# Running counts and scores of the second pass looked up in float32 from one table

## The reference

```python
src = jnp.concatenate([_s, _d, _loop]); dst = jnp.concatenate([_d, _s, _loop])
_o = jnp.argsort(dst, stable=True); src = src[_o]; dst = dst[_o]
...
def _L1_gnn_ref(node_states, edges, kernel, kernel_attention):
    dst = edges[:, 0]                      # edges = stack([src, dst], axis=1)
    src = edges[:, 1]
    h = jnp.matmul(node_states, kernel)
    score_dst = jnp.matmul(h, a_dst); score_src = jnp.matmul(h, a_src)
    scores = jax.nn.leaky_relu(score_dst[dst] + score_src[src], negative_slope=0.2)
    scores = jnp.exp(jnp.clip(scores, -2.0, 2.0))
    scores_sum = jax.ops.segment_sum(scores, dst, num_segments=n_nodes)
    attention_norm = scores / scores_sum[dst]
    return jax.ops.segment_sum(h[src] * attention_norm[:, None], dst, num_segments=n_nodes)
```

## Time and profile before

| | |
|---|---|
| median of the runs | 12312.5 us |
| the profiled execution | 12319.95 us, its span 12318.2 us |
| stage_move in its span | about 4041 to 7355 us |
| mean granted TensorE clock | 0.804 of 2.4 GHz |
| busy in the span | PE 6923.2 us, DVE 6711.3, POOL 6398.0, ACT 1613.7 |

### The profile page before, as it was taken

One profiled execution on the slowest core, in us unless ns is written; L12 is line 12 of the kernel. 1 busy time (PEld: TensorE's weight loads), 2 busy tenths in 40 slices (PEclk: granted clock), 3 DMA queues, 4 the chain that ended last, 5 costly groups with the idle time before them and its releaser, 6 DMA issues. The chain is left out here.

```text
span 12318.2 us, 202597 instructions
## 1 busy us (share of the span) xinstructions
PE 6923.2 (56%) x43540; PEld 5743.1 (47%) x43541; DVE 6711.3 (54%) x13147; ACT 1613.7 (13%) x4982; POOL 6398.0 (52%) x7772
## 2 busy tenths in 40 slices
PE   4777777776583555555555526996467730100375
PEld 3666666665473444444444424773256630000364
DVE  5333333334677555555555525887455689600499
ACT  1000000000211322222222200111100000000011
POOL 2555555551384344444444455882166678877300
PEclk9999999999797777777777758997588865555698
DMA  3555555553373344444444459993077742344454
GB/s 98 161 159 157 161 160 159 161 159 114 106 207 92 113 129 131 129 128 132 129 130 127 139 155 179 269 268 85 28 179 192 192 123 73 92 113 108 127 168 127
DMA packets 2114487, 1742.89 MB, mean 141 GB/s; under 512 B 377268, under 2 KB 1838645, under 8 KB 2114213
## 3 DMA queue, kind: packets, MB, share of 16 engines
q1 hardware_dynamic: 1220182, 819.70, 22.8%
q10 hardware_dynamic: 708032, 472.39, 15.8%
q0 software_dynamic: 186160, 449.72, 13.0%
HBM read 1289.54 MB, written 453.29 MB: 141 GB/s over the span
## 5 line engine op out<-in xcount | busy, mean ns | idle before, releaser
L1152 POOL DMA_INDIRECT sorted<-m_rows,srci x1612 | 1574.4, 977 | 1768.6 <-ACT srci L1256 978.0
L1612 POOL DMA_INDIRECT z_xg<-table,srci x1664 | 1888.1, 1135 | 725.5 <-issue 473.3
L452 POOL DMA_INDIRECT g_xg<-table,srci x1612 | 1581.1, 981 | 1105.8 <-DVE g_es L554 628.3
L1201 PE MATMUL m_psl<-m_part,m_ohtb 128*128 128x100 bf16 x4836 | 472.1, 251 | 1175.7 <-DVE m_mul L1340 725.7
L471 PE MATMUL g_psg<-g_wg,g_eT 128*128 128x136 f32 x3224 | 1047.0, 472 | 135.3 <-issue 134.3
L1672 PE MATMUL z_ps<-z_wrow,z_oh 128*128 128x132 f32 x3712 | 575.0, 302 | 957.8 <-issue 472.2
L488 PE MATMUL g_psx<-scores,g_hot 128*128 x3608 | 840.3, 362 | 446.1 <-DVE e_score L579 267.7
L488 PEld LDWEIGHTS g_psx<-scores,g_hot 128*128 128x128 f32 x3608 | 806.5, 328 | 477.8 <-issue 476.5
L1484 PE MATMUL n_ps<-n_row,n_oh 128*128 128x257 f32 x3712 | 880.3, 389 | 192.6 <-DVE n_row L1460 170.4
L1201 PEld LDWEIGHTS m_psl<-m_part,m_ohtb 128*128 128x128 bf16 x4836 | 408.5, 123 | 1227.3 <-issue 978.0
L1672 PEld LDWEIGHTS z_ps<-z_wrow,z_oh 128*128 128x128 f32 x3712 | 488.6, 203 | 1044.3 <-issue 972.9
(11 more groups left out here) (412 smaller groups left out, 13950.8 us busy)
## 6 DMA issues: line engine op xcount, KB each, us to landing
n_row<-sorted SPq DMA_DIRECT2D x464, 520.0 KB, 4.7
z_buf<-gathered ACTq DMA_DIRECT2D x464, 256.0 KB
g_keys<-dst_row ACTq DMA_DIRECT2D x451, 256.0 KB
ag_buf<-gated SPq DMA_DIRECT2D x451, 256.0 KB, 3.2
m_keys<-dst_row ACTq DMA_DIRECT2D x451, 256.0 KB
gathered<-z_xg SPq DMA_DIRECT2D x416, 256.0 KB
gated<-g_y SPq DMA_DIRECT2D x403, 256.0 KB
g_eT<-in_attr_t SPq DMA_DIRECT2D x402, 256.0 KB
```

The lines of the kernel that those rows point to most:

```text
L452: nc.gpsimd.indirect_dma_start(out=xg[:, u, j, :], out_offset=None, in_=v.table[:, :], in_offset=bass.IndirectOffsetOnAxis(ap=v.srci[:, t: ...
L1152: nc.gpsimd.indirect_dma_start(out=v.sorted[:, :], out_offset=bass.IndirectOffsetOnAxis(ap=place[:, t:t + 1], axis=0), in_=rows[:, u, j, : ...
L1201: nc.tensor.matmul(to, ohtb[:, u, j * P:(j + 1) * P], before, start=(n == 0), stop=False)
L1612: nc.gpsimd.indirect_dma_start(out=xg[:, u, j, :], out_offset=None, in_=v.table[:, :], in_offset=bass.IndirectOffsetOnAxis(ap=v.dsti[:, t: ...
```

## The change

The three bf16 terms go. `cnt` gets a second half with the score of every node, filled once, and `lookups` multiplies a float32 copy of the transposed one-hots, `oht`, with `cnt` directly: one float32 matmul of 100 columns for a tile where there were three in bf16. `ohtb` stays for `same`. The parts `high` and `middle` go from ACT, `below_high` and `below_middle` from DVE; `turned` gets a second copy from PSUM. `lookups` now waits for `s_qm`, `s_oht`, `s_run` and `s_mul`; `counts` also waits for the second copy of the group before; `running` waits for lookups of three groups earlier.

```diff
-        cnt, mul = sb("_cnt", [P, R, G, NBX]), sb("_mul", [P, 2, G, 2, NBX])
-        part, rest = sb("_part", [P, R, 3, G, 2, NBX], BF16), sb("_rest", [P, 2, G, NBX])
+        oht = sb("_oht", [P, R, G * P])
+        cnt, mul = sb("_cnt", [P, R, G, 2, NBX]), sb("_mul", [P, 2, G, 2, NBX])
...
                     if later(g, 1):
                         pe.wait_ge(s_run, g + 1)
                         pe.wait_ge(s_ohtb, g)
+                        pe.wait_ge(s_oht, g)
...
                 def lookups(g, u, use):
                     pe.wait_ge(s_qm, g + 1)
-                    pe.wait_ge(s_ohtb, g + 1)
-                    pe.wait_ge(s_low, g + 2)
+                    pe.wait_ge(s_oht, g + 1)
+                    pe.wait_ge(s_run, g + 2)
...
-                        for n in range(3):
-                            before = part[:, u, n, j - 1, :, :] if j else part[:, (u - 1) % R, n, G - 1, :, :]
-                            nc.tensor.matmul(to, ohtb[:, u, j * P:(j + 1) * P], before, start=(n == 0), stop=False)
+                        before = cnt[:, u, j - 1, :, :] if j else cnt[:, (u - 1) % R, G - 1, :, :]
+                        nc.tensor.matmul(to, oht[:, u, j * P:(j + 1) * P], before, start=True, stop=False)
                         last = nc.tensor.matmul(to, qm[:, u, j, :], ohhi[:, u, j, :, :], start=False, stop=True)
...
                     nc.scalar.activation(ohtb[:, u, :], pst[:, :], ACT.Copy).then_inc(s_ohtb, 1)
-
-                def high(g, u, use):
...
-                    nc.scalar.activation(part[:, u, 0, :, 0, :], cnt[:, u, :, :], ACT.Copy).then_inc(s_high, 1)
+                    nc.scalar.activation(oht[:, u, :], pst[:, :], ACT.Copy).then_inc(s_oht, 1)
...
-                def middle(g, u, use):
-                    act.wait_ge(s_rest, g + 1)
-                    nc.scalar.activation(part[:, u, 1, :, 0, :], rest[:, u % 2, :, :], ACT.Copy).then_inc(s_middle, 1)
...
+                nc.vector.tensor_copy(cnt[:, :, :, 1, :].rearrange("p r t c -> p (r t) c"),
+                                      v.scores[:, None, :, 0].broadcast_to([P, R * G, NBX])).then_inc(s_fix, 1)
...
                     if later(g, R):
-                        dve.wait_ge(s_rest, g - R + 1)
+                        dve.wait_ge(s_look, g - R + 2)
                     dve.wait_ge(s_cnt, g + 1)
-                    nc.vector.tensor_tensor(cnt[:, u, :, :], tiles(psu[:, 0:G * NBX]),
-                                            cnt[:, (u - 1) % R, G - 1:G, :].broadcast_to([P, G, NBX]),
+                    nc.vector.tensor_tensor(cnt[:, u, :, 0, :], tiles(psu[:, 0:G * NBX]),
+                                            cnt[:, (u - 1) % R, G - 1:G, 0, :].broadcast_to([P, G, NBX]),
                                             ALU.add).then_inc(s_run, 1)
-
-                def below_high(g, u, use):
...
-                def below_middle(g, u, use):
...
-                pipeline(dve, GE, (hot, 3, KE), (fill, 6, KE), (below_middle, 3), (choose, 4), (onehots, 0), (running, 1),
-                         (below_high, 2), (position, 4), ring=R)
+                pipeline(dve, GE, (hot, 3, KE), (fill, 6, KE), (choose, 4), (onehots, 0), (running, 1), (position, 4), ring=R)
```

More of the change, by code:

```diff
@@ L1090, in stage_move @@
     s_oh, s_cnt, s_run, s_ohtb = (sem("r_" + n) for n in ("oh", "cnt", "run", "ohtb"))
-    s_first = sem("r_first")
-    s_high, s_rest, s_middle, s_low = (sem("r_" + n) for n in ("high", "rest", "middle", "low"))
+    s_oht = sem("r_oht")
     s_q, s_qm, s_look, s_mul, s_pos, s_place = (sem("r_" + n) for n in ("q", "qm", "look", "mul", "pos", "place"))
@@ L1195, in lookups @@
                     else:
-                        pe.wait_ge(s_fix, R + 1)
+                        pe.wait_ge(s_fix, 2)
                     for j in range(G):
                         to = psl[:, j * 2 * NBX:(j + 1) * 2 * NBX]
-                        for n in range(3):
-                            before = part[:, u, n, j - 1, :, :] if j else part[:, (u - 1) % R, n, G - 1, :, :]
-                            nc.tensor.matmul(to, ohtb[:, u, j * P:(j + 1) * P], before, start=(n == 0), stop=False)
+                        before = cnt[:, u, j - 1, :, :] if j else cnt[:, (u - 1) % R, G - 1, :, :]
+                        nc.tensor.matmul(to, oht[:, u, j * P:(j + 1) * P], before, start=True, stop=False)
                         last = nc.tensor.matmul(to, qm[:, u, j, :], ohhi[:, u, j, :, :], start=False, stop=True)
@@ L1236, in turned @@
                     nc.scalar.activation(ohtb[:, u, :], pst[:, :], ACT.Copy).then_inc(s_ohtb, 1)
-                def high(g, u, use):
-                    act.wait_ge(s_run, g + 2)
-                    if later(g, R):
-                        act.wait_ge(s_look, g - R + 2)
-                    nc.scalar.activation(part[:, u, 0, :, 0, :], cnt[:, u, :, :], ACT.Copy).then_inc(s_high, 1)
+                    nc.scalar.activation(oht[:, u, :], pst[:, :], ACT.Copy).then_inc(s_oht, 1)
                 def earlier(g, u, use):
@@ L1266, in put @@
                                          facts[:, ds(g * G, G), 1:4], ACT.Copy).then_inc(s_put, 1)
-                pipeline(act, GE, (spread, 1, KE), (turned, 2), (high, 2), (earlier, 2), (middle, 3), (index, 5), (put, 5, KE), ring=R)
+                pipeline(act, GE, (spread, 1, KE), (turned, 2), (earlier, 2), (index, 5), (put, 5, KE), ring=R)
             @block.vector
@@ L1272, in _ @@
                 nc.vector.memset(rows[:, :, :, :], 1.0).then_inc(s_set, 1)
-                nc.vector.tensor_copy(cnt[:, R - 1, G - 1, :], run[:, :]).then_inc(s_run, 1)
+                nc.vector.tensor_copy(cnt[:, R - 1, G - 1, 0, :], run[:, :]).then_inc(s_run, 1)
                 link = chain(dve, s_split)
@@ L1318, in running @@
                     if later(g, R):
-                        dve.wait_ge(s_rest, g - R + 1)
+                        dve.wait_ge(s_look, g - R + 2)
                     dve.wait_ge(s_cnt, g + 1)
-                    nc.vector.tensor_tensor(cnt[:, u, :, :], tiles(psu[:, 0:G * NBX]),
-                                            cnt[:, (u - 1) % R, G - 1:G, :].broadcast_to([P, G, NBX]),
+                    nc.vector.tensor_tensor(cnt[:, u, :, 0, :], tiles(psu[:, 0:G * NBX]),
+                                            cnt[:, (u - 1) % R, G - 1:G, 0, :].broadcast_to([P, G, NBX]),
                                             ALU.add).then_inc(s_run, 1)
-                def below_high(g, u, use):
[L1326 to L1329, removed]
-                def below_middle(g, u, use):
-                    dve.wait_ge(s_middle, g + 1)
-                    nc.vector.tensor_tensor(part[:, u, 2, :, 0, :], rest[:, u % 2, :, :], part[:, u, 1, :, 0, :],
-                                            ALU.subtract).then_inc(s_low, 1)
                 def choose(g, u, use):
```

## The result

The changed kernel takes 11918.58 us, the kernel before beside it 12309.51 us: ratio 0.9684, 95% interval 0.9671 to 0.9696, 391 us less. The forecast was 12104 with 11780 to 12330. The sign and the place were right; the gain is nearly twice the sum.

What follows compares the result with a forecast made beforehand. stage_move was taken to be bound by POOL's own time plus the stretch from PE's late signals to its next burst. Gains of 180, 15, 11 and 2.5 us (set-up) sum to 209: 12104 us, range 11780 to 12330.

Steps and rivals of the forecast that it cites:

- What bounds the kernel: In stage_move no engine is full; it pays POOL's own time plus the stretch from signal release to next burst.
- The stretch after a release: In stage_move, from PE's late signals to POOL's restart: 5.85 us, shortened by 1.45 us a release; 206 us in all.
- The hand-over as a gain by itself: DVE's choose no longer waits through L1333 for ACT's second term behind its late copy: 1.17 us a release.
- DVE's two instructions: DVE loses L1328 and L1333; L1328's 0.28 us comes off the way from choose to fill.
- The slower rival: PE's expand signal is caught behind POOL's burst, so bursts of two groups break up; 12570 us, chance 0.12.
- The count being last nearly always: At DVE's L1321 the count's signal comes last nearly always, so an earlier choose waits; 12256 us, chance 0.12.
- a sign of no gain: In stage_move: waits of DVE's L1321 for PE grown from 53.
- PE as the end of the stretch: After a release PE at 1.2 GHz ends the stretch, its longer lookups uncovered; 12310 us, chance 0.10.
- PE's price: In lookups, float32 costs 0.6 us more a step, scaled from expand by columns; covered, so nothing in the sum.
- The scatters: On POOL: with fewer two-operand DVE instructions they come back a little to 960 ns; too small to enter.
- The larger gain: Stage_move's loop leaves the burst pattern: 588 us less, 11724, or about half, 12020; chance 0.15.

Runs made afterwards that it cites:

- e1_middle_first: Kernel before with ACT's part middle moved ahead of earlier, so the second bf16 term no longer queues behind the late copy; 12129 us, ratio 0.9992.
- e3_dve_work_back: Changed kernel with two DVE subtractions of 200 columns added per step, whose results nobody reads; 12063 us, ratio 0.9937.
- r_before: Kernel before, unchanged, run for its trace on a chip without late signals; 9697 us.
- r_after: Changed kernel, unchanged, run on a chip without late signals; 9677 us, ratio 0.9972.
- e5_fill_behind: Kernel before with fill moved behind below_middle on DVE; 12156 us, ratio 1.0011.

## Why the prediction was right, point by point

*What bounds the kernel* was read rightly for that chip: bursts, late signals, and a stage that pays for POOL plus the stretch to its restart. On the fast chips there are no late signals, POOL has no wait of this kind, and the stage takes 1161 us less.

*The stretch after a release* was the mis-sized term. The sum took 1.45 us off for 124 releases and less for the rest, 206 us in all; POOL's waits for others fell by 499 us over some 205 restarts, 2.4 us each. The step that failed is that a release would find DVE at the choose, with only 1.45 us less to do. These are the stretches from the end of DVE's longest wait to POOL's restart, grouped by where DVE stood (median in us, and the number of restarts in brackets, in the steps with lookups; the 11 to 29 restarts before which DVE had no wait over 1 us are left out):

| DVE stood at | before | after | e1_middle_first | e3_dve_work_back |
|---|---|---|---|---|
| the fill | 1.6 (3) | 1.6 (116) | 1.6 (39) | 1.6 (44) |
| the counts | 3.2 (12) | 3.2 (40) | 3.8 (66) | 3.2 (109) |
| the choose | none | 4.9 (22) | 4.9 (95) | 4.7 (35) |
| the third term, L1333 | 5.4 (165) | gone | 2.4 (2) | gone |

The stretch goes with the place and is much the same in all four. For the place that the prediction assumed, the choose, it is 4.9 us where 4.4 was forecast, but that is only 22 restarts of after. In most DVE rests at the fill, with the choose and its signals behind it; a fill then follows the release at once. What the sum left out on the other side is that the release comes later after the last scatter (1.51 against 0.27 us).

That the time fell inside the range is in part luck: 11919 lies outside 12020 to 12190, to which the forecast gave 0.48, and the range reached down to it for the sake of a rival with another mechanism.

*The hand-over as a gain by itself* (1.17 of the 1.45 us) did not show on chip 7: with it gone and DVE's work left, the time is the same, and the wait stands at the next signal of PE. *DVE's two instructions* were held to be worth 0.28 us a release. Their return left a gain of 78 us, in place of what would be some 380 if 0.968 holds there; that would be 0.75 us a step for 0.72 us of busy time. That the two parts act together is what the runs suggest. Why DVE comes to rest at the fill, which of PE's signals gets out ahead of the burst, is argued and not shown.

*The slower rival* named the right event and the wrong price. PE's expand did get caught behind the burst: that is the 149 waits of the fill. But its signal was late about as often before, over 1 us in 207 of 438 records of it, after in 211 of 417; DVE had to wait at the fill for it only 13 times before, since it stood elsewhere. A step that waits had its other work done, as the text said against this rival, and the fill comes first after the release. Counted from the scatters (a stop is over 1 us of idle time), bursts of four went from 15 to 38 and bursts of eight from 158 to 145, not a quarter of them.

*The count being last nearly always* did not happen. It is the commonest place of DVE in e3_dve_work_back (129 waits at the counts, 86 at the choose, 56 at the fill). In after the waits of the counts for PE doubled from 53 to 106, which was given as a sign of no gain; the gain came all the same. *PE as the end of the stretch* did not show in the result, although PE's price was too low: tiles follow each other at 5308.81 and 5309.40, so 0.59 us at 1.2 GHz against 0.33, 1.04 us a step and not 0.6, near the upper bound. Scaling the expand row by columns was wrong: by the same rows the float32 call of 100 columns takes some 0.51 us (an estimate, 0.59 less a quarter of 0.33 for the bf16 matmul beside it), and expand with 129 columns 0.52.

*The scatters* were left out of the sum as too small, and grew by 83 us. See below.

*The larger gain* (588 us, or half) is nearer to the truth than the forecast in its size: 391 us, and half of it had been put at 12020. Its mechanism, a loop without bursts, did not come: POOL still stops some 200 times.

## What to carry to other kernels

Where several engines wait on each other in a ring, find at which instruction each of them stands when a delay ends; what counts is how much work lies between that instruction and the one that feeds the bound engine, and taking one wait away can just move the stop to the next signal. Don't take a stall that the profile puts down to "remote" for a property of the kernel until a second chip shows it: here the stage took 3314 us with it and 2153 without, and the gain was 3.2% with it and 0.25% without. Before costing work as hidden, ask by which resource it could still slow the bound engine.

## What the runs showed of the hardware

*PE's signals come late on some chips and not on others.* The trace records when a semaphore is updated, with some updates missing. In stage_move of before 787 of 1615 updates by PE came over 1 us after the end of its instruction, for "same" 179 of 394, with a median of 6.1 and at most 12.0 us, for expand at most 15.4. Of 4643 updates by ACT and DVE in the same stretch none came over 0.02 us after. In r_before and r_after all 3221 updates by PE came within 0.02 us. The windows above add that the late ones cost time in stages with POOL's indirect DMAs: in stage_move and the first stage, and not in the one behind stage_move, which has none and shows no wait for "remote". On the chips where they come, PE's own float32 instructions also come slowly at such times: in after, matmuls of L1209 begin 0.7 to 1.4 us apart.

```profile
5303.83 0.27 PE L1209 MATMUL m_psx<-held,m_hot 128*128 x1 [0.18 <-issue]
...
5305.25 0.27 PE L1209 MATMUL m_psx<-held,m_hot 128*128 x1 [1.16 <-issue]
5306.01 0.27 PE L1209 MATMUL m_psx<-held,m_hot 128*128 x1 [0.48 <-issue]
```

The ends of matmuls in the trace are modelled, so a late signal may be a late product. What delays them stays open.

*A scatter that starts early in a DVE instruction with two SBUF operands is longer.* In the release above the scatter of 1.40 us starts at 5308.47, inside L1282 (from 5308.35, 0.69 us), which reads iota and lo from SBUF. Counted over the trace of after, 168 scatters take over 1.3 us, and all 168 start inside an L1282, 164 of them at a restart; before it was 1 of 1, in e5_fill_behind 291 of 291. Beside L1303, which reads one operand from SBUF and one from PSUM, they take 0.96 us (153 of them). So the new rhythm, in which POOL restarts just as DVE builds the next one-hots, costs about 0.4 us a restart, some 75 of the 83 us. The Trainium skill has the rule (SBUF — State Buffer, "Who interferes with whom": a DVE instruction with two SBUF inputs contends with a GpSimd instruction that reads SBUF); this trace agrees and puts the price at 1.40 against 0.96 us. It isn't the whole of it: scatters that start inside the comparison of keys, L1317, which reads one tensor, take 1.09 us on average (199 of them), and before, inside L1354, as much (107); why stays open.
